# Storing the result of an RWKV and mixture-of-experts layer in eight pieces, each after its own last add, instead of in one

## The chip, the cores and the metric

The kernel runs on all 8 cores of one Trainium2 chip. Each core computes one element of the batch, with its own copy of all weights, and there is no traffic between cores. The metric is the device time of the slowest core, in microseconds. On each core TensorE (PE), VectorE (DVE), ScalarE (ACT), GpSimd (POOL) and SyncE (SP) run their own instruction streams and meet through semaphores; SP does nothing here but issue DMAs.

## The reference

The reference takes x of shape (8, 2048, 1024) and applies two blocks, each to a layer norm of its input and with a residual add. Cut to what matters:

```python
x = x + rwkv_attn(_layernorm(x))     # k, v, r projections, WKV scan over t, output projection
x = x + ffn(_layernorm(x))

# ffn: 15 experts and an identity expert, top 2 of 16, and a shared branch with a causal conv gate
routed = combine[:, E - 1:E] * flat
for e in range(E - 1):
    y = jax.nn.silu(flat @ expert_gate_w[e]) * (flat @ expert_up_w[e]) @ expert_down_w[e]
    routed = routed + combine[:, e:e + 1] * y
shared = jax.nn.silu(gate) * (hidden_states @ shared_up_w) @ shared_down_w
return shared + routed
```

All 15 experts are computed for all tokens; `combine` is zero where a token has not chosen the expert.

## The kernel before

On each core x stands transposed, channels by tokens, in one tile `acc` of 128 partitions by 8 by 2048 in f32. Channel c is partition c mod 128 of piece c div 128, and a piece is called `cc` or `oc`. `acc` holds x from the start, is added to in place by every part of the layer, and is the output in the end: 64 KB in each partition, 8192 KB in all. `outv` is the output tensor in DRAM seen in the same shape; there, one piece `oc` is 128 rows of 2048 f32 values (8 KB each), which lie one behind the other.

The first block (lines 100 to 387) is the attention part, over four slices of 512 tokens. SP loads x there with four DMAs (line 179), and VectorE casts each slice (line 199). Then come the second layer norm, the router (whose result `cfm` SP stores to DRAM at line 595, 128 KB) and the expert part.

The expert part is a loop over 15 experts on each engine. For expert e TensorE forms gate (line 702) and up (line 716) in four pieces of 128 inner channels, all 2048 tokens at once in four PSUM banks; ScalarE applies silu (line 800), VectorE multiplies (lines 770 and 771) into `h`. Then TensorE forms the down product (line 728): for each of the eight `oc` 16 matmuls, four for each of four groups of tokens, into one of two halves of PSUM. When one `oc` is through, VectorE adds its four banks into `acc[:, oc, :]` with four instructions of 512 tokens each (line 779), and notes the count of its semaphore `s_dv` after the fourth under the name `v:dadd{e}_{oc}`. TensorE may use a half of PSUM again once the adds of two `oc` before are done. Weights of the next experts are loaded by GpSimd (line 655) into four slots, each when its last reader is done; for the last experts nothing is left to load.

The order of the work is written out by hand: each engine's program is a list, and waits on `s_pe`, `s_dv` and `s_sc` hold it together. The end of the kernel is on SP, in the block of the expert part: it waits for the last add of the last expert, `v:dadd14_7` (line 806), stores all of `acc` with one DMA (line 807), and waits for the DMA's completion on `s_do` (line 808; a DMA adds 16 to its semaphore when it is complete).

Of the kernel before, what the change touches and what calls it, by code (L numbers as in the profile page):

```python
# [13 lines left out]
CC = 8  # L14
L = 128
NTC = T // L
NE = 15
# [41 lines left out]
def build_one(ms, rec, stop_after="ffn", taps=(), parts=("id", "sh", "ex")):  # L59
    nc = bass.Bass("TRN2", target_bir_lowering=False)  # L60

    def MS(key):
        return 0 if rec else ms[key]
# [18 lines left out]
    tap_d = {}  # L82
# [6 lines left out]
    outv = out_d.rearrange("(cc p) t -> p cc t", p=128)  # L89

    with ExitStack() as st:
        en = st.enter_context
        acc = en(nc.sbuf_tensor("acc", [128, CC, T], F32))
# [6 lines left out]
        s_dv = en(nc.semaphore("s_dv"))  # L100
# [10 lines left out]
        s_do = en(nc.semaphore("s_do"))  # L111
# [13 lines left out]
        with ExitStack() as s1:  # L125
# [24 lines left out]
            @blk.gpsimd  # L150
            def _(g):
                GS.eng = g

                def wload(m):
                    wsrc = [wk_d, wv_d, wr_d, wo_d]
                    if m >= 4 * NSC:
                        return
                    if m >= 2:
                        g.wait_ge(s_pe, MS(f"t:MAT{m - 2}"))
                    g.dma_start(wsl_a[m % 2][:],  # L160
                                wsrc[m % 4].rearrange("(cc p) d -> p cc d", p=128)
                                ).then_inc(s_dwa if m % 2 == 0 else s_dwb, 16)

                g.dma_start(par[:], par_d[:]).then_inc(s_dpar, 16)
                g.dma_start(id_sb[:], id_d[:]).then_inc(s_dpar, 16)
                wload(0)
                wload(1)
                for s_ in range(NSC):
                    wload(4 * s_ + 2)
                    wload(4 * s_ + 3)  # L170
                    wload(4 * s_ + 4)
                    wload(4 * s_ + 5)
# [246 lines left out]
        with ExitStack() as s2:  # L419
            e2 = s2.enter_context  # L420
            ln2x = e2(nc.sbuf_tensor("ln2x", [128, CC, T + 2], BF16))
# [189 lines left out]
            with ExitStack() as sb4:  # L611
# [190 lines left out]

                @blk4.sync
                def _(sy):
                    n_do = 1 + ("comb" in tap_d) + ("ln2x" in tap_d)
                    sy.wait_ge(s_dv, MS(f"v:dadd{NE - 1}_7"))
                    sy.dma_start(outv, acc[:]).then_inc(s_do, 16)
                    sy.wait_ge(s_do, 16 * n_do)

    return nc  # L810
# [45 lines left out]
```

## Time and profile before

| | us |
|---|---|
| two timed runs | 2965.94 and 3092.89, median 3029.41 |
| the profiled execution | 2864.96 |
| its span on the slowest core (core 1) | 2863.4 |
| spans of the eight cores | 2847.5 to 2863.4 |

The profiled execution is one run of the program with the hardware profiler on; its span goes from the first to the last instruction of core 1. It is a run of its own, faster than the two that were timed without a profile. Line numbers are those of the kernel before. In what follows, times in the rows are microseconds from the start of the span unless they are marked ns.

### The profile page before, as it was taken

To read this page: it belongs to the slowest core of one execution; us is meant where nothing else is said; L and a number is where in the kernel's file an instruction comes from. 1 tells how busy PE (TensorE), PEld (TensorE's weight loads), DVE (VectorE), ACT (ScalarE), POOL (GpSimd) and SP (SyncE) were. 2 spreads that over 40 slices of the span, in tenths; PEclk is the share of its full clock that TensorE was granted. 3 is DMA by queue.
4 is the path that set the end of the run, shared out by engine and by line. 5 is a ranking of instruction groups with operands and counts; after the bars stand their busy time and mean duration, and the time that the engine had idled before them with its cause. 6 is when DMAs were issued, how large, how long until landed. Compare 5 with 4: busy or idle time off the path is not lost.

```text
span 2863.4 us, 21636 instructions; the slowest of 8 cores (2847.5 to 2863.4 us)
## 1 busy us (share of the span) xinstructions
PE 1867.5 (65%) x7648; PEld 783.3 (27%) x7648; DVE 1278.7 (45%) x1772; ACT 327.0 (11%) x551; POOL 67.9 (2%) x88
## 2 busy tenths in 40 slices
PE   3415424226032678887887887888878878878885
PEld 1102101102010333333333333333333333333332
DVE  4574574584458532243342442442433424424433
ACT  0310220310410000100101001001001010010010
POOL 0000000000010000000000000000000000000000
PEclk8757757667566889898998998989988889989887
DMA  7603404305026000032132131221321321312203
GB/s 148 90 28 50 67 0 62 56 0 88 0 36 96 17 8 1 1 52 37 15 52 37 15 50 22 33 37 15 52 37 15 52 37 15 47 22 35 30 1 118
DMA packets 69195, 112.79 MB, mean 39 GB/s; under 512 B 2480, under 2 KB 37312, under 8 KB 68048
## 3 DMA queue, kind: packets, MB, share of 16 engines
q0 software_dynamic: 63856, 94.50, 22.5%
q1 hardware_dynamic: 5232, 16.91, 1.8%
q8 instruction: 62, 1.02, 0.1%
q14 instruction: 45, 0.37, 0.0%
HBM read 197.28 MB, written 8.52 MB: 72 GB/s over the span
## 4 chain that ended last, share of the span: by engine, by line
PE 53%; DVE 10%; issue 2%; ACT 1%; DVEq 0%; DMA 0%; ACTq 0%; POOLq 0%
PE pc L702 18%; PE pc L728 16%; PE pc L716 15%; DVE h L771 4%; DVE sg L770 4%; PE pc L667 2%; PE pc L686 1%; ACT sg L800 1%; PE pc L675 1%; DVE h L741 1%; DVE acc L744 1%; DVE acc L779 0%; DVE h L753 0%; DVEq L36 0%; DMA cb<-comb_dram 0%
## 5 line engine op out<-in xcount | busy, mean ns | idle before, releaser
L702 PE MATMUL pc<-ln2x,wsl 128*128 128x512 bf16 x1920 | 522.6, 439 | 191.0 <-ACT sg L800 189.9
L770 DVE TENSOR_TENSOR sg<-sg,pc 128x512 f32<-128x512 f32 x240 | 165.0, 687 | 825.3 <-PE pc L716 806.3
L728 PE MATMUL pc<-h,wsl 128*128 128x512 bf16 x1920 | 461.4, 404 | 100.6 <-DVE h L771 99.9
L716 PE MATMUL pc<-ln2x,wsl 128*128 128x512 bf16 x1920 | 427.6, 379 | 0.0
L779 DVE TENSOR_TENSOR acc<-acc,pc 128x512 f32<-128x512 f32 x480 | 330.1, 688 | 182.8 <-PE pc L728 144.2
L702 PEld LDWEIGHTS pc<-ln2x,wsl 128*128 128x128 bf16 x1920 | 207.2, 110 | 505.2 <-issue 345.5
L800 ACT ACTIVATE sg<-pc 128x512 f32<-128x512 f32 x240 | 143.4, 597 | 1525.1 <-PE pc L702 1019.0
L728 PEld LDWEIGHTS pc<-h,wsl 128*128 128x128 bf16 x1920 | 190.4, 103 | 371.6 <-issue 191.8
L369 PE MATMUL pb<-mx,wsla 128*128 128x512 bf16 x512 | 131.0, 424 | 241.7 <-DVE mx L225 215.4
L716 PEld LDWEIGHTS pc<-ln2x,wsl 128*128 128x128 bf16 x1920 | 187.6, 98 | 230.2
L771 DVE TENSOR_TENSOR h<-sg,cb 128x512 bf16<-128x512 f32 x240 | 166.1, 692 | 25.4 <-DVE sg L770 0.5
L369 PE MATMUL pb<-sry,wsla 128*128 128x512 bf16 x256 | 63.7, 415 | 143.0 <-DVE sry L282 94.9
L369 PEld LDWEIGHTS pb<-mx,wsla 128*128 128x128 bf16 x512 | 54.0, 107 | 318.6 <-issue 271.0
L369 PE MATMUL pb<-mxb,wsla 128*128 128x512 bf16 x256 | 61.4, 405 | 65.1 <-DMA wsla<-wv 58.5
L667 PE MATMUL pc<-ln2x,cw_sb 128*128 128x512 bf16 x384 | 86.2, 386 | 9.6 <-PEq L517 6.4
L360 PE MATMUL pb<-xb,ones_b 128*128 128x512 bf16 x32 | 13.5, 598 | 102.8 <-DVE xsq L200 102.8
L369 PEld LDWEIGHTS pb<-sry,wsla 128*128 128x128 bf16 x256 | 26.6, 105 | 180.1 <-issue 155.4
L271 DVE TENSOR_TENSOR_SCAN P_ch<-ewb,P_ch,w 128x128 f32<-128x128 f32 x128 | 62.0, 484 | 13.7 <-DVE P_ch L271 0.5
L275 DVE TENSOR_TENSOR_SCAN Q_ch<-ewb,Q_ch,e_t 128x128 f32<-128x128 f32 x128 | 62.0, 484 | 13.7 <-DVE Q_ch L275 0.5
L260 DVE CAST v_sb<-pb 128x512 bf16<-128x512 f32 x32 | 22.1, 692 | 97.6 <-PE pb L369 94.7
L281 DVE TENSOR_TENSOR w<-w,e_t 128x1024 f32<-128x1024 f32 x16 | 19.6, 1225 | 95.8 <-ACT e_t L328 95.8
L369 PEld LDWEIGHTS pb<-mxb,wsla 128*128 128x128 bf16 x256 | 26.1, 103 | 100.3 <-issue 74.2
(121 smaller groups left out, 908.6 us busy)
## 6 DMA issues: line engine op xcount, KB each, us to landing
wsl<-gw POOLq DMA_DIRECT2D x15, 1024.0 KB, 9.5
wsl<-uw POOLq DMA_DIRECT2D x15, 1024.0 KB, 10.1
wsl<-dw POOLq DMA_DIRECT2D x15, 1024.0 KB, 10.6
acc<-x SPq DMA_DIRECT2D x4, 2048.0 KB, 25.0
wsla<-wk POOLq DMA_DIRECT2D x4, 2048.0 KB, 17.1
wsla<-wv POOLq DMA_DIRECT2D x4, 2048.0 KB, 18.6
wsla<-wr POOLq DMA_DIRECT2D x4, 2048.0 KB, 29.2
wsla<-wo POOLq DMA_DIRECT2D x4, 2048.0 KB, 17.2
```

What stands on the lines that cost most here:

```text
L271: VS.do(lambda cc=cc: v.tensor_tensor_scan(P_ch[:, cc, 1:], ewb[:, cc, :], w1[:, cc, :], P_ch[:, cc, 0:1], OP.mult, OP.add))
L275: VS.do(lambda cc=cc: v.tensor_tensor_scan(Q_ch[:, cc, 1:], ewb[:, cc, :], e_t[:, cc, :], Q_ch[:, cc, 0:1], OP.mult, OP.add))
L369: inst = t.matmul(pb[od][:], wsl_a[m % 2][:, kc, od * 128:(od + 1) * 128], rhs_t[:, kc, :], start=(kc == 0), stop=(kc == CC - 1))
L667: inst = t.matmul(pc4[ocI][:], cwS[:, kk * 8 + kc, ocI * 128:(ocI + 1) * 128], ln2x[:, kc, t0 - 2 + kk: t0 - 2 + kk + 512], start=(kk == 0 ...
L675: inst = t.matmul(pc4[4 + ocI][:], suS[:, kc, ocI * 128:(ocI + 1) * 128], ln2x[:, kc, t0:t0 + 512], start=(kc == 0), stop=(kc == CC - 1))
L702: inst = t.matmul(pc4[tc][:], slot_ap(3 * e)[:, kc, ocI * 128:(ocI + 1) * 128], ln2x[:, kc, 2 + tc * 512: 2 + (tc + 1) * 512], start=(kc = ...
L716: inst = t.matmul(pc4[4 + tc][:], slot_ap(3 * e + 1)[:, kc, ocI * 128:(ocI + 1) * 128], ln2x[:, kc, 2 + tc * 512: 2 + (tc + 1) * 512], sta ...
L728: inst = t.matmul(pc4[(oc % 2) * 4 + tc][:], slot_ap(3 * e + 2)[:, kcI, oc * 128:(oc + 1) * 128], h[:, kcI, tc * 512:(tc + 1) * 512], star ...
L770: VS.do(lambda sl=sl, tc=tc: v.tensor_tensor(sl[:], sl[:], pc4[4 + tc][:], OP.mult))
L771: VS.do(lambda sl=sl, e=e, ocI=ocI, tc=tc: v.tensor_tensor(h[:, ocI, tc * 512:(tc + 1) * 512], sl[:], cb[e % 2][:, tc, :], OP.mult), f"h{e ...
L779: VS.do(lambda dst=dst, ac=ac, oc=oc, tc=tc: v.tensor_tensor(dst, ac, pc4[(oc % 2) * 4 + tc][:], OP.add))
L800: SS.do(lambda idx=idx, tc=tc: s.activation(sg[idx % 2][:], pc4[tc][:], AF.Silu), f"silu{e}_{ocI}_{tc}")
```

## The change

The one store of `acc` becomes a loop over the eight `oc`. For each, SP waits until VectorE has done the four adds of the last expert into that piece, and stores the piece. The final wait is for all eight completions. `taps` is empty in the kernel that runs, so `n_do` is 1 before and 8 after.

```diff
                 @blk4.sync
                 def _(sy):
-                    n_do = 1 + ("comb" in tap_d) + ("ln2x" in tap_d)
-                    sy.wait_ge(s_dv, MS(f"v:dadd{NE - 1}_7"))
-                    sy.dma_start(outv, acc[:]).then_inc(s_do, 16)
+                    n_do = 8 + ("comb" in tap_d) + ("ln2x" in tap_d)
+                    for oc in range(CC):
+                        sy.wait_ge(s_dv, MS(f"v:dadd{NE - 1}_{oc}"))
+                        sy.dma_start(outv[:, oc, :], acc[:, oc, :]).then_inc(s_do, 16)
                     sy.wait_ge(s_do, 16 * n_do)
```

## Rows read from the trace of the kernel before

**Rows 1.** The page: span, busy time of the engines, chain that ended last by engine

```profile
span 2863.4 us, 21636 instructions; the slowest of 8 cores (2847.5 to 2863.4 us)
...
PE 1867.5 (65%) x7648; PEld 783.3 (27%) x7648; DVE 1278.7 (45%) x1772; ACT 327.0 (11%) x551; POOL 67.9 (2%) x88
...
PE 53%; DVE 10%; issue 2%; ACT 1%; DVEq 0%; DMA 0%; ACTq 0%; POOLq 0%
```

**Rows 2.** Cores: span and mean granted TensorE clock, longest and shortest core

```profile
core 1: 2863.4 us, clock 0.817
core 2: 2847.5 us, clock 0.818
...
core 5: 2862.3 us, clock 0.815
```

**Rows 3.** Timeline of core 1's end: start, us, engine, line, operation [idle before <-releaser]

```profile
2805.35 30.80 PE L728 MATMUL pc<-h,wsl 128*128 128x512 bf16 x128 [6.64 <-DVE h L771]
...
2811.88 3.06 DVE L779 TENSOR_TENSOR acc<-acc,pc 128x512 f32<-128x512 f32 x4 [6.67 <-PE pc L728]
...
2815.33 3.06 DVE L779 TENSOR_TENSOR acc<-acc,pc 128x512 f32<-128x512 f32 x4 [0.39 <-PE pc L728]
...
2818.88 3.06 DVE L779 TENSOR_TENSOR acc<-acc,pc 128x512 f32<-128x512 f32 x4 [0.48 <-PE pc L728]
...
2836.33 3.06 DVE L779 TENSOR_TENSOR acc<-acc,pc 128x512 f32<-128x512 f32 x4 [0.39 <-PE pc L728]
2839.48 0.39 SPq L807 DMA_DIRECT2D out<-acc  x1
```

**Rows 4.** Waits of SP on core 1: total us, times, longest

```profile
SPq L806 <- DVE acc L779: 1873.7, 1, 1873.7
...
SPq L808 <- DMA out<-acc: 23.2, 1, 23.2
```

**Rows 5.** Windows of core 1's end: window, us, busy us by engine, clock, DMA share, GB/s

```profile
2805.30:2839.50 34.20, 30.80 (x128) 12.73 (x128) 22.00 (x32) 0.00 (x0) 0.00 (x0) 0.90 0.00 0
2839.50:2863.40 23.90, 0.00 (x0) 0.00 (x0) 0.00 (x0) 0.00 (x0) 0.00 (x0) 0.50 0.93 351
...
2844.00:2857.50 13.50, 0.00 (x0) 0.00 (x0) 0.00 (x0) 0.00 (x0) 0.00 (x0) 0.50 1.01 357
```

**Rows 6.** DMA issues of core 1: how many, KB of each, median us to landing

```profile
wsl<-gw POOLq DMA_DIRECT2D x15, 1024.0 KB, 9.5
...
out<-acc SPq DMA_DIRECT2D x1, 8192.0 KB, 23.6
...
comb_dram<-cfm SPq DMA_DIRECT2D x1, 128.0 KB, 2.6
```

**Rows 7.** The store on core 3 and on core 4, issue to landing

```profile
DMA to landing us min/median/max: 22.2/22.2/22.2
...
DMA to landing us min/median/max: 25.1/25.1/25.1
```

**Rows 8.** DMA issues of core 1 between 130 and 160 us

```profile
acc<-x SPq DMA_DIRECT2D x1, 2048.0 KB, 10.1
```

**Rows 9.** Line 199 (ns min/median/max), and windows over its first and last call

```profile
L199 DVE CAST xb<-acc x4: 2294/2294/2295, 18.4 to 540.0; 128x4096 bf16<-128x4096 f32 x4
...
18.40:20.70 2.30, 0.00 (x0) 0.00 (x0) 2.26 (x1) 0.00 (x0) 0.00 (x0) 1.00 0.98 209
540.00:542.30 2.30, 0.00 (x0) 0.00 (x0) 2.25 (x1) 2.02 (x4) 0.00 (x0) 0.50 0.00 0
```

**Rows 10.** Line 779 (ns min/median/max), and a window with a weight load beside it

```profile
L779 DVE TENSOR_TENSOR acc<-acc,pc x480: 686/687/690, 1234.9 to 2838.7; 128x512 f32<-128x512 f32 x160
...
2611.40:2614.60 3.20, 3.20 (x17) 1.46 (x15) 2.40 (x4) 0.00 (x0) 0.88 (x1) 1.00 0.47 41
```

## The prediction

> **What bounds the kernel now.** I read the page first, for the span and the chain that ended last. The chain is 53% TensorE and 10% VectorE, with DMA at 0% [rows 1]; but the span closes at 2863.4 us and the last compute instruction ends long before, so the end had to be looked at by itself. The view of cores shows that no core is far out: core 1 is the longest with 2863.4 us, core 2 the shortest with 2847.5 us, at clocks of 0.817 and 0.818 [rows 2]. A tail common to all eight cores is therefore worth its full length.
>
> The timeline of the last stage of core 1 shows what the diff touches [rows 3]. The down products of the last expert start at 2805.35 and take 30.80 us. VectorE adds them into `acc` in eight groups of four, one for each `oc`: the first starts at 2811.88 and ends 3.06 us later, at 2814.94, the following ones start at 2815.33 and 2818.88 (spacings 3.45 and 3.55 us, 3.5 on average), and the last starts at 2836.33 and ends at 2839.39. At 2839.48, which is 0.09 us after it, SP issues the one store of all of `acc`. The waits of SP say the same from the other side: it stood 1873.7 us at line 806 for the last add, and then 23.2 us at line 808 for the store [rows 4]. In those last 23.9 us the windows show no compute instruction on any engine, and DMA engines at a share of 0.93 with 351 GB/s; in the 34.2 us before, during the down products, the DMA share is 0.00 [rows 5]. So the end of the kernel is a pure store, behind a stretch in which the DMA engines have nothing at all to do.
>
> **The change, part by part.** It removes one store of 8192 KB and adds eight of 1024 KB, each of which waits for the four adds of its own `oc`. No instruction of TensorE, VectorE, ScalarE or GpSimd changes; SP gets seven more waits and seven more issues. Nothing else is queued on SP in this stage: its only work there is this store [rows 4], so no engine waits behind the added waits. The final wait is for eight completions instead of one.
>
> *Issues.* The issue of the large store takes 0.39 us on SP [rows 3]. Eight of them, one each 3.5 us, take 8 x 0.39 = 3.1 us in total, of which seven lie beside the down products. The eighth is issued at 2839.48, when the single store was issued before: it adds nothing. If nothing covered the seven, they would cost 2.7 us.
>
> *One chunk.* No row shows a store of 1024 KB, so I take it from two rows of the same SP queue in the same direction: 128 KB land 2.6 us after their issue, 8192 KB land in 23.6 us [rows 6]. That is (23.6 - 2.6) us for 8064 KB, or 2.60 us for each 1000 KB, so 1024 KB move in 2.67 us; the fixed part is 2.6 us less the 0.33 us of its 128 KB, or 2.27 us. One chunk alone lands 2.27 + 2.67 = 4.9 us after its issue. The bounds: from below 2.6 us, the landing of the 128 KB store, since eight times the bytes can't be faster. From above, the nearest row of another kind is the last load of `x` on the same queue, 2048 KB in 2 KB pieces, in 10.1 us [rows 8]; half its time above the fixed part gives (10.1 - 2.27)/2 = 3.9 us of transfer and 6.2 us in all. The weight loads of 1024 KB issued by GpSimd take 9.5 us [rows 6], but they convert from f32 and come through another queue. I take 4.9, because the two stores it comes from have the same queue, direction and 8 KB rows.
>
> *The queue before the last chunk.* What counts is when the eighth lands, and so whether the seven before it are out of the way. The first can be issued at 2814.94 + 0.09 = 2815.03, the next ones every 3.5 us. A transfer of 2.67 us fits in 3.5 us, which leaves the DMA engines idle about a quarter of the time; at 2839.48 the seventh, issued 3.5 us earlier, has moved its bytes or nearly so. The eighth then lands at 2839.48 + 4.9 = 2844.4. Before, the large one landed at 2839.48 + 23.6 = 2863.1. The gain is 18.7 us. With the lower bound of a chunk it is 23.6 - 2.6 = 21.0 us. With 3.9 us of transfer the DMA engines are always behind (3.9 against 3.5): the last bytes move at 2815.03 + 2.27 + 8 x 3.9 = 2848.5, a gain of 14.6 us.
>
> The Trainium skill ("SBUF — State Buffer", section "The DMA setup-cost knee (why "@ 1 MiB" ≠ asymptote)") states about 2 us fixed for a DMA plus the bytes at 436 GB/s. By that estimate a chunk is 4.4 us and the gain 19.2 us; for the large store the same rule gives 21.2 us where the trace has 23.6, so it is a little fast here.
>
> *Neighbours.* The stores now run while TensorE reads `h` and the weights, and VectorE reads and writes `acc`. What hides them is that these engines don't mind. The trace has cases of it: the cast of `acc` at line 199 takes 2294 to 2295 ns in all four of its calls, the first with 209 GB/s of DMA beside it, the last with 0 [rows 9]. The adds of line 779 take 686 to 690 ns in all 480 calls, some of them with loads of weights beside them (DMA share 0.47) [rows 10]. So I cost this at nothing. The price if it is not nothing is a rival below.
>
> *Other cores.* The store lands in 22.2 us on core 3 and in 25.1 on core 4 [rows 7], while others store too. Each core gains its own landing less 4.9 us: 17.3 to 20.2. The slowest core before, core 1, stays the slowest or gives way to core 5 at about the same time.
>
> **The sum.** 2864.96 us is the time of the profiled execution (its span is 2863.4). 2864.96 - 18.7 = 2846.3 us, that is -0.65%. The two timed runs shown are 2965.94 and 3092.89 us, median 3029.41: the profiled execution is 164 us or 5.4% below that median, and the two differ by 4.3%. The tail saved is a transfer, which doesn't grow with a slower TensorE clock, so I take the same 18.7 us off: 3029.41 - 18.7 = 3010.7 us.
>
> **The rivals.**
> *The fixed part is paid by each chunk in turn.* If a store on one queue doesn't begin before the one ahead of it has landed, chunks come every 4.9 us, not every 3.5: 2815.03 + 8 x 4.94 = 2854.5, a gain of 8.6 us, 3020.8 us. For it: no row shows two stores of this queue in flight together. Against: within the large store the rate stays at 357 GB/s and more in the middle [rows 5], so the engines themselves run on from row to row. The Trainium skill speaks against the change here ("SBUF — State Buffer", same section): it says to coalesce into the largest single transfer, because of the fixed cost. That is this rival; whether chunks overlap their fixed part no row of before shows.
>
> *Chunks are slow, and the end is later than before.* The eight land before 2863.1 only if each takes less than (2863.1 - 2815.03)/8 = 6.0 us in turn. At the 9.5 us of a 1024 KB weight load [rows 6] the last would land at 2891.0, 27.9 us later: 3057.3 us. It needs stores of this queue at 110 GB/s, where the large one ran at 351 over its whole window [rows 5], and the small one took 2.6 us.
>
> *The stores slow the adds.* VectorE has 3.06 us of adds in each 3.5 us, about 0.4 to spare. To eat up the 18.7 us each of the eight groups would have to be 18.7/8 = 2.3 us longer, 5.8 us, and so each add some 1.3 us instead of 0.69. From there on the kernel is slower than before; at adds of 0.8 us the loss is under 1 us and the gain about 18. The 2294 and 2295 ns of line 199 speak against any such thing [rows 9]. At twice the add (1.37 us, groups of about 5.9 us) the end would be 0 to 1 us later: 3030 us.
>
> **How the numbers follow.** The forecast, a gain of 14 to 21 us, has 0.80; the serial chunks 0.10; late chunks 0.04; slowed adds 0.03; something not thought of 0.03. None of them reaches 2% (about 57 to 61 us, and about what a measurement of this kernel can tell from no change): that would take more than the whole tail of 23.9 us. What is left over for faster and slower comes from the measurement, whose runs of one kernel lie 4.3% apart and, with the profiled one, between 2865 and 3093. So: faster 0.10, same 0.85, slower 0.05, more on the side to which the gain shifts it. For the range the same spread decides: the lowest time seen less the largest gain is 2864.96 - 21.0 = 2844, taken as 2840; the highest less the smallest gain is 3092.89 - 8.6 = 3084, taken as 3080. The change by itself, against the same kind of run, is -21 to -8 us.
>
> **What would show it.** On each core the last store lands about 4.9 us after its issue, and SP's wait for it falls from 23.2 to about 4.6 us; the eight issues stand 3.5 us apart, the first right after the first four adds; the DMA share in the down stage rises from 0.00 to 0.6 or 0.8; line 779 stays at 686 to 690 ns and the down products at 30.8 us. The step on the queue is wrong if the last landing takes 10 us or more: the serial rival says 15. The step on neighbours is wrong if the adds or the down stage are longer. The whole is wrong if the stretch before the last add changes at all.

## The result and the profile after

The changed kernel takes 2844.93 us (median of 27 runs), the one before 2865.0 us (median of 26). The ratio is 0.9937 with a 95% interval of 0.9925 to 0.9949, that is 18 us less, between 15 and 21. Of the 26 runs of the kernel before, 16 lie between 2861.7 and 2867.0 us and ten lie 2% to 9% above, the two shown ahead (2965.94 and 3092.89) among them; the ratio leaves such long runs out, in which (in the changed kernel) one die shows a granted TensorE clock down to 0.73 where the other shows 0.82.

The profiled execution of the changed kernel has a span of 2843.7 us on its slowest core, which is core 3 now. First the page, then the waits of SP and rows of the timeline (columns as in [rows 4] and [rows 3]):

```profile
span 2843.7 us, 21650 instructions; the slowest of 8 cores (2829.0 to 2843.7 us)
```

```profile
SPq L807 <- DVE acc L779: 1867.8, 8, 1846.2
...
SPq L809 <- DMA out<-acc: 4.3, 1, 4.3
```

```profile
2804.64 30.81 PE L728 MATMUL pc<-h,wsl 128*128 128x512 bf16 x128 [6.64 <-DVE h L771]
2811.17 3.06 DVE L779 TENSOR_TENSOR acc<-acc,pc 128x512 f32<-128x512 f32 x4 [6.68 <-PE pc L728]
2814.32 24.77 SPq L808 DMA_DIRECT2D out<-acc  x8
...
2835.63 3.06 DVE L779 TENSOR_TENSOR acc<-acc,pc 128x512 f32<-128x512 f32 x4 [0.39 <-PE pc L728]
```

The single wait of 23.2 us [rows 4] is now 4.3 us, and this is nearly all of the gain: the span is 19.7 us shorter, the wait 18.9 us. The first store is issued at 2814.32, 0.09 us after the end of the first four adds (2811.17 + 3.06), the last 24.5 us later. The down products take 30.81 us, where they took 30.80 [rows 3].

The line that issues the stores, with its landings, and line 779 (ns min/median/max):

```profile
L808 SPq DMA_DIRECT2D out<-acc x8: 332/332/368, 2814.3 to 2838.8; - x8
...
DMA to landing us min/median/max: 3.9/4.0/5.7
```

```profile
L779 DVE TENSOR_TENSOR acc<-acc,pc x480: 686/687/690, 1234.1 to 2838.0; 128x512 f32<-128x512 f32 x160
```

The windows show how one piece goes (columns as in [rows 5]; the first two windows in whole stages, then single microseconds):

```profile
2814.30:2838.80 24.50, 21.15 (x97) 8.97 (x96) 19.24 (x28) 0.00 (x0) 0.00 (x0) 0.97 0.73 299
2838.80:2843.70 4.90, 0.00 (x0) 0.00 (x0) 0.00 (x0) 0.00 (x0) 0.00 (x0) 0.50 0.54 221
...
2814.00:2815.00 1.00, 1.00 (x6) 0.32 (x4) 0.61 (x2) 0.00 (x0) 0.00 (x0) 1.00 0.00 0
2815.00:2816.00 1.00, 1.00 (x6) 0.49 (x5) 0.90 (x2) 0.00 (x0) 0.00 (x0) 1.00 0.94 393
2816.00:2817.00 1.00, 1.00 (x7) 0.42 (x5) 0.79 (x2) 0.00 (x0) 0.00 (x0) 1.00 0.96 393
2817.00:2818.00 1.00, 1.00 (x6) 0.40 (x5) 0.69 (x1) 0.00 (x0) 0.00 (x0) 1.00 0.64 262
2818.00:2819.00 1.00, 1.00 (x6) 0.47 (x5) 0.72 (x2) 0.00 (x0) 0.00 (x0) 1.00 0.55 229
```

Bytes flow from about 2815.0, 0.7 us after the issue, at some 400 GB/s until about 2817.6; the landing is counted at 2818.2 to 2818.3. So a piece is 0.7 us, then 2.6 us of bytes, then 0.6 us until it counts as landed. The DMA share of the stage in which the stores hide is 0.73, where the whole down stage had 0.00 [rows 5].

### The profile page after: what moved, and what is told of

Read it like the earlier page. It is cut to its first block, busy times and chain, and to the rows that moved or that the text cites. A ratio compares the mean times of both kernels' runs of the same rounds, so it can differ in the third digit from the quotient of the medians.

```text
span 2843.7 us, 21650 instructions; the slowest of 8 cores (2829.0 to 2843.7 us)
## 1 busy us (share of the span) xinstructions
PE 1872.4 (66%) x7648; PEld 784.0 (28%) x7648; DVE 1278.7 (45%) x1772; ACT 327.0 (11%) x551; POOL 67.9 (2%) x88
## 4 chain that ended last, share of the span: by engine, by line
PE 53%; DVE 10%; issue 2%; ACT 1%; DVEq 0%; DMA 0%; ACTq 0%; POOLq 0%
PE pc L702 18%; PE pc L728 16%; PE pc L716 15%; DVE h L771 4%; DVE sg L770 4%; PE pc L667 2%; PE pc L686 1%; ACT sg L800 1%; PE pc L675 1%; DVE acc L744 1%; DVE h L741 1%; DVE acc L779 0%; DVE h L753 0%; DVEq L36 0%; DMA cb<-comb_dram 0%
## 5 line engine op out<-in xcount | busy, mean ns | idle before, releaser
L369 PE MATMUL pb<-mxb,wsla 128*128 128x512 bf16 x256 | 67.2, 432 | 65.1 <-DMA wsla<-wv 58.6
```

Source lines behind the costliest of these rows:

```text
L369: inst = t.matmul(pb[od][:], wsl_a[m % 2][:, kc, od * 128:(od + 1) * 128], rhs_t[:, kc, :], start=(kc == 0), stop=(kc == CC - 1))
```

## The experiments

All are edits of the loop of the changed kernel on SP; all other engines are left as they are. The number of completions that the final wait asks for, `n_do`, is set to the number of stores in each; that line is left out of the diffs. Each ratio is that of the run to the kernel before, timed on the same chip, with its 95% interval. "Issue to landing" is the time from the issue of one DMA until it has landed.

**Is the gain the early issue or the cutting, and do pieces behind one another overlap?** All eight are issued back to back after the last add.

```diff
+                    sy.wait_ge(s_dv, MS(f"v:dadd{NE - 1}_7"))
                     for oc in range(CC):
-                        sy.wait_ge(s_dv, MS(f"v:dadd{NE - 1}_{oc}"))
                         sy.dma_start(outv[:, oc, :], acc[:, oc, :]).then_inc(s_do, 16)
```

> The eight pieces as in the changed kernel, but all issued back to back after the last add: the store is cut, not moved. Theory (the gain is the early issue, and pieces behind one another on the queue overlap their fixed part): eight issues of 0.33 us, transfers of 2.8 us each behind one another, last landing 23 to 25 us after the first issue, time that of the kernel before (2864, within 3 us). Serial rival (a piece starts only when the one ahead has landed, 4.0 us each): 32 us, time about 2872, that is 8 us slower than before. If cutting by itself were the gain, the time would be near 2845.

The ratio to the kernel before is 1.0003 (0.9992 to 1.0013), so cutting by itself gives nothing. On its slowest core (core 2), timeline and then waits of SP:

```profile
2843.71 8.29 SPq L808 DMA_DIRECT2D out<-acc  x8
```

```profile
SPq L809 <- DMA out<-acc: 16.5, 1, 16.5
```

From the first issue to the last landing it is 8.29 + 16.5 = 24.8 us, and 23.7 to 24.9 us over the eight cores, where the one large store had 22.2 to 25.1 [rows 6, 7]. Eight landings of 3.9 us one after the other would be 31 us. Pieces on one queue do overlap; the serial rival falls. What was new is the issue:

```profile
L808 SPq DMA_DIRECT2D out<-acc x8: 368/1250/1260, 2843.7 to 2850.7; - x8
```

Right behind one another most issues take 1.25 us of SP, where 3.5 us apart they take 0.33. SP has nothing else to do, and the bytes of the pieces ahead take longer than that, so it costs nothing here.

**How does the landing of the last piece go with its size?** Two stores of 4096 KB, and four of 2048 KB, each after the last add of its part.

```diff
-                    for oc in range(CC):
-                        sy.wait_ge(s_dv, MS(f"v:dadd{NE - 1}_{oc}"))
-                        sy.dma_start(outv[:, oc, :], acc[:, oc, :]).then_inc(s_do, 16)
+                    for oc in (0, 4):
+                        sy.wait_ge(s_dv, MS(f"v:dadd{NE - 1}_{oc + 3}"))
+                        sy.dma_start(outv[:, oc:oc + 4, :], acc[:, oc:oc + 4, :]).then_inc(s_do, 16)
```

> Two stores of 4096 KB, the first after oc 3, the second after oc 7. The landings 4.0 us (1024 KB) and 23.6 us (8192 KB) give a line of 2.8 us for each 1024 KB and a fixed part of 1.2 us. Theory: the second store lands 12.4 us after its issue, time 2864 - 11.2 = 2853. With the fixed part of my prediction (2.27 us, 2.67 us for 1024 KB) it would be 12.9 us and 2853.5. If the gain were nothing but the first start of the stores, it would be the same as with eight pieces, 2845.

The same with `oc` in steps of two gives the four pieces:

> Four stores of 2048 KB, each after two oc. With 1024 KB in 3.9 us, 4096 KB in 12.0 and 8192 KB in 23.6, a line of 2.8 us for each 1024 KB and 1.1 us fixed gives 6.7 us for the last one, and a time 2.8 us above that of eight pieces, 2848. Rival (landing does not go by the bytes, since the queue is what is waited for): 3.9 us or 12 us.

The DMA issues of the two kernels (how many, KB of each, median us to landing), two pieces and then four:

```profile
out<-acc SPq DMA_DIRECT2D x2, 4096.0 KB, 12.0
```

```profile
out<-acc SPq DMA_DIRECT2D x4, 2048.0 KB, 6.5
```

The ladder is 3.9 us for 1024 KB, 6.5 for 2048, 12.0 for 4096 (11.4 to 13.1 over the cores), 23.6 for 8192. The first step is 2.6 us for 1024 KB, and 3.9 - 2.6 = 1.3 us remain as the fixed part. The steps are not all alike: the next ones are 2.75 and 2.9 us for 1024 KB. That agrees with the rates: one piece alone moves at 393 GB/s and more, the large store at 349 to 393 in windows of 5 us. Against the kernel before, two pieces have a ratio of 0.9953 (0.9929 to 0.9977), 13 us less (7 to 20) where 11 were expected; four have 0.9951 (0.9935 to 0.9967), 14 us less (9 to 19). The order of the sizes is read from the landings; of the ratios only that with one store or with eight late ones lies apart, since 2.6 us are 0.1%.

**Would finer pieces at the end gain more?** The store of oc 7 is cut in four by tokens, each part after its own add, and in another kernel in two.

```diff
-                    for oc in range(CC):
+                    for oc in range(CC - 1):
                         sy.wait_ge(s_dv, MS(f"v:dadd{NE - 1}_{oc}"))
                         sy.dma_start(outv[:, oc, :], acc[:, oc, :]).then_inc(s_do, 16)
+                    for tc in range(4):
+                        tsl = slice(tc * 512, (tc + 1) * 512)
+                        sy.wait_ge(s_dv, max(1, MS(f"v:dadd{NE - 1}_7") - 3 + tc))
+                        sy.dma_start(outv[:, CC - 1, tsl], acc[:, CC - 1, tsl]).then_inc(s_do, 16)
```

> Seven pieces as in the changed kernel, and the last oc in four pieces of 256 KB, each after its own add. Theory with a fixed part of 1.2 us and 2.8 us for 1024 KB: the last piece lands 1.9 us after its issue, 2.1 us earlier than now, time 2843. If the fixed part is the 2.27 us of my prediction: 2.9 us, gain 1 us, 2844. Serial rival: the four pieces, issued 0.79 us apart, are taken one by one at 2 to 3 us each, the last lands 6 to 9 us after its issue, and the time is 2847 to 2850.

Ratio 0.994 (0.9923 to 0.9958), no better than the changed kernel. The parts land 3.9 us after their issue (the median on core 2, the slowest), though they have a quarter of the bytes. SP's last wait is 3.1 us there and 3.1 to 5.6 us over the cores. The windows of core 2 say why:

```profile
2838.00:2839.00 1.00, 0.00 (x0) 0.00 (x0) 0.90 (x2) 0.00 (x0) 0.00 (x0) 1.00 0.62 262
2839.00:2840.00 1.00, 0.00 (x0) 0.00 (x0) 0.90 (x2) 0.00 (x0) 0.00 (x0) 0.90 1.10 451
...
2842.00:2843.00 1.00, 0.00 (x0) 0.00 (x0) 0.00 (x0) 0.00 (x0) 0.00 (x0) 0.50 1.05 311
2843.00:2844.00 1.00, 0.00 (x0) 0.00 (x0) 0.00 (x0) 0.00 (x0) 0.00 (x0) 0.50 0.95 307
```

The DMA engines are full from about 2838.4 to 2844.0: the 1024 KB of oc 6 are still moving when the first part of oc 7 comes, and the last parts, in rows of 2 KB, go at about 310 GB/s where a whole piece had 393. That this is due to the short rows is not shown: on core 4 two windows of the same phase have only 182 and 125 GB/s, at DMA shares of 1.26 and 1.03, and several stores are under way at once. Neither my theory (1.9 us) nor the serial rival (6 to 9 us) held as a number: the queue was not empty, which the theory had taken for granted. Hence two halves with rows of 4 KB:

> Seven pieces as in the changed kernel, and oc 7 in two halves of 512 KB (4 KB rows), each after its two adds. In the run with four pieces of 256 KB the DMA engines were full from the issue of oc 6 to the end. Bytes alone set a bound: the 2048 KB of oc 6 and 7 need 2 x 2.5 us from 0.7 us after the issue of oc 6, and 0.7 us to land: 6.3 us after that issue, against 3.55 + 3.9 = 7.4 us now. Theory (bytes are the bound, halves keep the full rate): last landing about 2.8 us after the last issue, 1.1 us less than now. Rival (a fixed part of 3 us or more whatever the size, as the 256 KB pieces might be read): 3.7 to 3.9 us, no gain.

The landings of the two halves and of the seven whole pieces on the slowest core (5), and SP's last wait there:

```profile
out<-acc SPq DMA_DIRECT2D x7, 1024.0 KB, 3.9
out<-acc SPq DMA_DIRECT2D x2, 512.0 KB, 3.1
```

```profile
SPq L813 <- DMA out<-acc: 2.6, 1, 2.6
```

On cores 5 and 6 the last half lands 2.9 us after its issue, as the bytes allow (2.6 + 0.33). On the others the last wait is 3.1 to 4.2 us, against 3.5 to 4.3 in the changed kernel run beside it. The rates differ by core here too: in single microseconds the halves move at 422 and 406 GB/s on core 5, and at 258 and 266 on core 0. In time the two can't be told apart: 0.9942 (0.9928 to 0.9956) against 0.9944 (0.9924 to 0.9964) for the changed kernel on the same chip. Whether halves are worth half a microsecond stays open; more than that they don't bring.

> The changed kernel itself, beside the others on one chip: last piece lands in 3.9 to 4.7 us, ratio to the kernel before 0.993, time about 20 us less. It is the measure for the three others of this call.

Its pieces land in 3.9 us (median), and its ratio of 0.9944 is the one given above.

**Do the early stores disturb the other engines?** Each piece is stored twice, the second time into a scratch tensor.

```diff
                         sy.dma_start(outv[:, oc, :], acc[:, oc, :]).then_inc(s_do, 16)
+                        sy.dma_start(scrv[:, oc, :], acc[:, oc, :]).then_inc(s_do, 16)
```

> Each piece is stored twice, once into the output and once into a scratch tensor in DRAM (16 MB in all), so the DMA engines are full through the down stage. Theory (stores don't touch the engines' work): adds of line L779 stay at 686 to 690 ns and the down products at 30.8 us; only the end is later, since 16 transfers of 2.8 us follow one another from the first issue: 24.5 us of early time hold less than 9 of them, last landing 20 to 22 us after the last issue, time 2861 to 2864. Rival (stores slow the adds or the matmuls): adds above 700 ns in the last stage, a down stage longer than 31 us, and a time above that.

The down products and the adds (here lines 730 and 781, since two lines come before), and the windows of the down stage from the first store on, and of the end, on core 6:

```profile
2809.02 30.80 PE L730 MATMUL pc<-h,wsl 128*128 128x512 bf16 x126 [6.64 <-DVE h L773]
```

```profile
L781 DVE TENSOR_TENSOR acc<-acc,pc x480: 686/687/690, 1238.5 to 2842.4; 128x512 f32<-128x512 f32 x160
```

```profile
2818.70:2843.10 24.40, 21.07 (x96) 8.96 (x96) 19.25 (x28) 0.00 (x0) 0.00 (x0) 0.98 0.98 351
2843.20:2868.20 25.00, 0.00 (x0) 0.00 (x0) 0.00 (x0) 0.00 (x0) 0.00 (x0) 0.50 0.94 327
```

With the DMA engines at a share of 0.98 and 351 GB/s beside them, the adds keep their 686 to 690 ns, and the down products take 30.80 us as before. The end is what the bytes make it: the last landing is 24.4 us after the last issue on this core and 21 to 24 us on the others, where 20 to 22 were expected, and the ratio is 0.9998 (0.9977 to 1.0018). Twice the bytes, half of them hidden, take the time of the kernel before.

**Do the seven early ones cost anything?** Only oc 7 is stored.

```diff
-                    for oc in range(CC):
-                        sy.wait_ge(s_dv, MS(f"v:dadd{NE - 1}_{oc}"))
-                        sy.dma_start(outv[:, oc, :], acc[:, oc, :]).then_inc(s_do, 16)
+                    sy.wait_ge(s_dv, MS(f"v:dadd{NE - 1}_7"))
+                    sy.dma_start(outv[:, CC - 1, :], acc[:, CC - 1, :]).then_inc(s_do, 16)
```

> Only the piece of oc 7 is stored, after the last add; the stores of the other seven are left out (seven eighths of the output are missing). Theory (the seven early stores cost nothing anywhere): the last piece lands 3.9 us after its issue, time within 1 us of the changed kernel on the same chip. Rival (the seven early ones hold up the last, or slow the down stage): faster than the changed kernel by what they cost; the 5.7 us seen as the longest landing of a piece would point to 1 to 2 us.

Its ratio is 0.9945 (0.9929 to 0.9960), against 0.9944 for all eight on the same chip. The one piece lands in 4.1 us on the slowest core, in 3.9 to 4.2 on all:

```profile
out<-acc SPq DMA_DIRECT2D x1, 1024.0 KB, 4.1
```

The seven are free within what can be measured here, some 4 us by these intervals. SP's last wait is finer: 3.5 to 3.8 us here, against 3.5 or 3.6 on six cores with all eight stores and 4.3 on the two others.

The 4.3 us have a cause of their own, and it answers the 5.7 us of the expectation. In the changed kernel and in this repeat of it, 5 of the 16 cores have a piece that lands in 5.7 to 5.9 us instead of 3.9, and a last wait of 4.3 or 4.4 us; the 11 others have no landing over 4.2 and a last wait of 3.5 or 3.6. On exactly those five, one packet of 16 KB of another queue moves while that piece does. On core 3 of the changed kernel, between 2837.5 and 2839.0 (queue: packets, MB, share of the 16 engines):

```profile
q1 hardware_dynamic: 66, 0.42, 70.1%
q8 instruction: 1, 0.02, 3.8%
```

By its name that queue loads instructions. The packet takes 3.8% of 16 engines for 1.5 us, that is 0.9 us of one engine. The trace counts a store as landed when all 16 DMA engines have ended their part; here 15 have ended at 2838.85 and the last one 1.6 us later. The longest landings with four pieces (8.3 us on core 5) and with halves (5.6 us for a whole piece on core 7) go with such a packet as well. So the 0.8 us of longer last wait are not a cost of the seven stores by themselves; why 0.9 us of one engine go with a landing that is 1.8 us late, these runs don't show.

## Why the prediction was right and where it failed

**The tail and its cover: right.** The end before was a pure store, and its length is what was gained: predicted 18.7 us, measured 18 (15 to 21) by the ratio, 18.9 us in SP's last wait of the profiled executions. That moving the stores ahead is the cause, and not cutting them, is shown by the eight late pieces (ratio 1.0003). That 18.7 and 18 are so close says little of the sum's parts: the landing in it was 1.0 us too long, and the ratio can't tell 18.7 from 19.7 us, which is what the spans of the two profiled executions differ by.

**The landing of one piece: right in kind, too long by a quarter.** I had 4.9 us, made of 2.27 fixed and 2.67 for the bytes; it is 3.9, made of 1.3 and 2.6. The term for the bytes was right. The fixed part was wrong because I drew the line through the store of 128 KB [rows 6], which is another shape: 16 partitions with one row of 8 KB each. It lands in 2.6 us, although one fixed part and its bytes at the rate of the others would be 1.3 + 0.3 = 1.6 us. So the line through two sizes held only among pieces of 128 partitions; why the 128 KB take longer is not shown. The estimate from the Trainium skill ("SBUF — State Buffer", section "The DMA setup-cost knee (why "@ 1 MiB" ≠ asymptote)"), 4.4 us, lay between: its 2 us fixed is more, and its time for the bytes (2.4 us) less, than the 1.3 and 2.6 us of the ladder here; the section says itself that its formula overstates the cost at middle sizes.

**The rivals: fallen, each with a run.** Pieces don't wait for one another's landing (24.8 us for eight, not 31). With it falls my use of the rule in the Trainium skill ("SBUF — State Buffer", the same section), to coalesce into the largest single transfer, as a reason against this change: eight pieces back to back cost as much as one store (24.8 us against 22.2 to 25.1), and the rule says nothing of what can be hidden. Slow pieces didn't come (3.9 us, not 9.5), and adds are not slowed even at a DMA share of 0.98. Two readings in the rivals were off without changing a chance: 357 GB/s is the mean over the middle of the large store [rows 5], and from 2850 to 2855 it is 349, so "and more" is too much; and only seven groups of adds come after the first store, so each would have to be 2.7 us longer, not 2.3.

**The absolute time: the step that failed.** It is the last step of the sum, "so I take the same 18.7 us off: 3029.41 - 18.7 = 3010.7 us". The kernel takes 2844.93 us, 166 us less, and 164 of these are the base: the kernel before takes 2865.0 us (median of 26 runs), not 3029.41. The gain in the sum was right to 1 or 2 us. My other sum, 2864.96 - 18.7 = 2846.3 us, made on the profiled execution, is 1.4 us from the result. I had three times of one kernel that lie up to 8% apart, and I took the median of the two that had no profiler on, and read their distance as the spread of the measurement. The runs show that the lowest of the three is the usual time: 16 of 26 lie within 0.2% of each other around it, and the two timed runs are among the ten above. The range of 2840 to 3080 was built on the same spread, and holds the result only near its lower end.

**The resolution, from the same error.** I wrote that a measurement of this kernel can tell about 2%, and took the chances of faster (0.10) and slower (0.05) from the distance of the two timed runs. The interval of the ratio is 0.12% to each side, so a gain of 0.65% is told clearly from none, though it stays under 2%, as I had it. The 0.05 for slower had no mechanism behind it: my rivals for a later end had 0.07 together, and by my own sums none of them reached 2%.

## What to carry to other kernels

Look at the last microseconds of the span by themselves. A store of everything behind the last add is worth its whole length less the landing of one last piece, the chain of waits can show it with 0% as here [rows 1], and it is removed by storing each part when it is final. The last part need only be small against that tail, and the earlier ones must be drained before it comes: a piece has to move in less time than the next one takes to be computed (2.6 us against 3.5 here; with twice the bytes the whole gain was gone). And where the times of one kernel lie further apart than the gain, find out which of them is usual before putting a gain on one; here it was the lowest, the profiled one.

## What the runs showed of the hardware that I had not expected

- An issue on SP takes 0.33 us when the one before it was 3.5 us earlier, and mostly 1.25 us right behind another. In the run with doubled stores the issue right behind took 0.43 to 1.27 us, and the next one, some 2 us later, 0.34 although stores were waiting by then; what sets it was not settled.
- A store of 128 partitions costs 1.3 us beside its bytes; a store of 128 KB from 16 partitions lands in 2.6 us.
- One piece of 1024 KB moves at 393 to 418 GB/s; the large store, eight pieces back to back and the doubled stores move at 344 to 393 in windows of 3 to 5 us once they are under way. Stores in rows of 2 KB and 4 KB, issued on the heels of others, went at anything between 125 and 426 GB/s with the DMA engines full, depending on the core; what sets that was not settled.
- A 16 KB packet on an instruction queue, 0.9 us on one DMA engine, goes with a landing that is 1.7 to 2.0 us late, in each of the seven cases where one came while the bytes of a store were moving (three cores of the changed kernel, two of its repeat, one each with halves and with four pieces).
